# Norms, 1x1 convolutions and a sparse mixture of experts: logits in eight 64x32 tiles over two banks, a spread per piece of the logits, a ring of five pieces, and the sums of steps 0, 2, 5 and 6 at other places

## Chip, cores and metric

One NeuronCore of one Trainium2 chip runs the kernel. The metric is device time in microseconds (us), of a whole execution.

## The reference

The input `x` is 8 images of 64 channels by 128x128 pixels, all fp32. First a convolution block, whose FFT and inverse cancel out:

```
xc = layernorm over channels of x
xn = groupnorm(8 groups)(xc) * gn_w + gn_b
x1 = x + xc + w2 @ relu(w1 @ xn + b1) + b2          # 1x1 convolutions
```

Then a sparse mixture. The reference reads x1 as (batch 8, tokens 16384, 64), normalizes each token over its channels, and computes

```
logits = tokens @ gate_w.T + gate_b                 # 32 experts
probs  = softmax over the 16384 tokens of an image
top 8 tokens of each expert, pooled with their probabilities
each expert's two-layer gelu network on the pooled vector
x1 += expert output * probability, at the chosen tokens
```

## The kernel before

**Layout.** An image lies in SBUF as 128 partitions (two halves of the pixels, `h`, times 64 channels) by 8192 columns, in `xs[it % 2]`. It is worked on in eight units `u` of 1024 columns (two slices `sl` of 512, each of two parts `sub` of 256). Two units make a group `m` for sums, and two units make a piece of the logits.

**Rounds and steps.** The main loop has eight rounds `it` of eight steps `s`. Every engine runs its own `step(it, s)`, in program order, and waits on semaphores. In round `it`, image `it` goes through its convolutions, image `it` + 1 is normalized (C jobs: subtract the mean; S jobs: multiply by the reciprocal deviation), and of image `it` - 1 the logits are scaled and the best tokens are found (L jobs in rounds 1 to 7, E jobs for the last image).

**PE in a step.** `conv1` (L383) of unit `s`; eight transposes into the two banks of `tl` (L400, for the stored tokens) of the unit before; a spread (L494); sums over channels; `conv2` (L391); a spread; the logits (L409) of the unit before; further sums. `spread_at(it, (s, j))` is the j-th spread of a step. A spread is four matmuls that copy a row of statistics over partitions into the two banks `bc`; DVE multiplies or subtracts it (L938, L940, L936) and only then may the next spread be written.

**Sums.** `sum_group` (L372) sums a group over the channels with 8 matmuls of 128x32 tiles: `x_sums` of the input and `xc_square_sums` of ACT's squares for the first norm, `x1_sums` and `x1_square_sums` for the token norm. The last waits for `sqx_done`, ACT's squares of x1 (L781). The square sums of group 1 need units 0 to 3 squared, and stood in step 5.

**The other engines.** DVE: statistics, the multiplies, `x1` (L948: adds the residual to `conv2`'s result), `max` and `max_index` of each piece (L1030, L1035), candidates (L1042 ff.). ACT: relu (L761), copies of tokens (L766) and logits (L776), squares (L794, L801, L781), exponentials (L806). POOL: adds (L1426), and gathers and scatters at the end. SP: loads and stores. ACT's order in a step:

```
relu(it, par, s)
square_at(it, (s - 1, 2));  explog(...);  token_copy(b, u)
square_at(it, (s, 0))
square_x1(b, b % 2, u)
logits_copy(b, u)
square_at(it, (s, 1))
```

with `u` = `s` - 1 for `s` from 1 on. `square_at(it, (4, 0))` is the square of the S0 job, which waits for DVE's multiply of S0. SP loads group `m` of image `it` + 2 in step 2m + 3 once `grp_done` says that the sums of squares of that group are done, and stores each unit's tokens after ACT's copy. In the prologue DVE builds constants, among them `spread`, while the first load is under way. After the loop come the last image's top tokens and the expert networks.

## Time and profile before

| | |
|---|---|
| median of 3 runs | 632.74 us (632.73 to 635.37) |
| the profiled execution | 639.6 us, span 637.9 us |
| mean granted TensorE clock | 0.935 |
| `x1` of step 0 in rounds 3, 4, 5, 6 | 248.65, 313.86, 379.05, 444.24 us |

The sums of the prediction are made against the profiled execution. The steps of round 4, by PE's start of `conv1`, and how long three engines were busy in each:

| step | from us | length | PE | DVE | ACT |
|---|---|---|---|---|---|
| 0 | 308.30 | 9.35 | 8.22 | 6.88 | 6.89 |
| 1 | 317.65 | 8.20 | 7.38 | 7.58 | 5.97 |
| 2 | 325.85 | 8.54 | 7.35 | 7.17 | 5.22 |
| 3 | 334.39 | 8.48 | 8.25 | 7.19 | 7.57 |
| 4 | 342.87 | 9.36 | 7.62 | 9.15 | 6.26 |
| 5 | 352.23 | 7.60 | 6.56 | 7.29 | 7.28 |
| 6 | 359.83 | 7.27 | 6.93 | 5.78 | 7.27 |
| 7 | 367.10 | 6.39 | 6.19 | 5.31 | 5.30 |

An engine that is busy for all of a step sets its length; where none is, the step is a chain of waits among them. The granted clock is 1.00 in all of these steps.

### The profile page before, as it was taken

How to read it: one execution, taken by the hardware profiler on the slowest of the kernel's cores; microseconds unless marked ns; L12 is line 12 of the kernel's file. 1: busy time of each engine (PE TensorE's matmuls, PEld its weight loads, DVE VectorE, ACT ScalarE, POOL GpSimd, SP SyncE). 2: the span in 40 equal slices, each digit the busy share in tenths (PEclk: the TensorE clock that was granted, in tenths of full speed). 3: DMA queues.
4: the chain of work that ended last, by engine and by line, in shares of the span. 5: the costliest groups of instructions: out<-in, count | busy, mean ns of one | idle time of the engine just before them, and what ended most of it. 6: DMA issues, size and time to landing. Idle time of an engine off the chain costs nothing.

```text
span 637.9 us, 14170 instructions
## 1 busy us (share of the span) xinstructions
PE 535.4 (84%) x5732; PEld 270.3 (42%) x5732; DVE 487.2 (76%) x950; ACT 435.3 (68%) x651; POOL 189.6 (30%) x116
## 2 busy tenths in 40 slices
PE   2749999898998899889989899989887988876982
PEld 1324444444444344444444444444443433434762
DVE  5574556689888988898789878988888687799620
ACT  2463779677976797679767976797677855984110
POOL 1007435023502260217020802080207145121144
PEclk9955999999999999999999999999998998987595
DMA  8960144714471447244634454445401255430000
GB/s 195 195 144 0 68 133 142 188 68 133 133 199 67 134 133 191 76 133 134 168 98 134 115 160 123 133 101 165 133 35 67 76 182 154 146 100 5 6 15 19
DMA packets 26752, 73.38 MB, mean 115 GB/s; under 512 B 4152, under 2 KB 4152, under 8 KB 22592
## 3 DMA queue, kind: packets, MB, share of 16 engines
q1 hardware_dynamic: 25664, 71.44, 40.9%
q0 software_dynamic: 1024, 1.05, 0.6%
q8 instruction: 45, 0.74, 0.5%
q14 instruction: 19, 0.16, 0.1%
HBM read 38.40 MB, written 34.08 MB: 114 GB/s over the span
## 4 chain that ended last, share of the span: by engine, by line
PE 41%; DVE 30%; ACT 13%; issue 12%; DMA 2%; POOL 1%; SPq 0%; ACTq 0%; DVEq 0%; POOLq 0%
PE st L372 11%; ACT junk L801 7%; DVE xs L948 7%; PE cv L383 6%; PE cv L391 6%; PE tl L400 6%; PE bc L494 5%; DVE us L938 5%; DVE lg L936 3%; DVE top_i L1035 2%; ACT tok L766 2%; DVE us L940 2%; DVE cnd L1030 2%; DMA xs<-in_x 2%; PE tl L409 2%
## 5 line engine op out<-in xcount | busy, mean ns | idle before, releaser
L1426 POOL TENSOR_TENSOR xs<-xs,us 128x1024 f32<-128x1024 f32 x64 | 151.2, 2379 | 367.2 <-DVE xs L948 173.4
L948 DVE SCALAR_TENSOR_TENSOR xs<-cv,vecs,xs 128x1024 f32<-128x1024 f32 x64 | 82.1, 1282 | 47.8 <-PE cv L391 47.7
L794 ACT ACTIVATE sqc<-us 128x1024 f32<-128x1024 f32 x64 | 67.5, 1054 | 46.2 <-DVE us L938 45.4
L761 ACT ACTIVATE hid<-cv,b1n 128x1024 f32<-128x1024 f32 x64 | 71.2, 1113 | 36.5 <-PE cv L383 36.0
L938 DVE TENSOR_TENSOR us<-xs,bc 128x1024 f32<-128x1024 f32 x60 | 73.0, 1216 | 19.7 <-PE bc L494 19.3
L400 PEld LDWEIGHTS tl<-ident,xs 128*128 128x128 f32 x512 | 63.8, 195 | 53.9 <-issue 53.9
L372 PE MATMUL st<-xs,stat_w 128*32 128x256 f32 x1024 | 74.5, 413 | 10.5 <-DMA xs<-in_x 9.4
L801 ACT ACTIVATE junk<-us 128x1024 bf16<-128x1024 f32 x64 | 67.3, 1051 | 22.8 <-DVE gsum L940 22.1
L940 DVE CUSTOM_DVE_ANT_0 us<-us,bc 128x1024 f32<-128x1024 f32 x60 | 72.9, 1215 | 11.2 <-PE bc L494 9.9
L400 PE MATMUL tl<-ident,xs 128*128 128x128 f32 x512 | 76.4, 294 | 0.9 <-ACT lg L776 0.9
L409 PE MATMUL tl<-xs,gcen 128*32 128x256 f32 x1024 | 69.4, 389 | 8.0 <-ACT tok L766 7.9
L494 PE MATMUL bc<-rstd_s,spread 32*128 32x256 f32 x368 | 48.2, 340 | 32.9 <-DVE gsum L940 20.3
L383 PE MATMUL cv<-us,w1n 64*64 64x512 f32 x512 | 72.1, 634 | 2.4 <-DVE b1n L1003 1.9
L391 PE MATMUL cv<-hid,w2bd 64*64 64x512 f32 x512 | 70.6, 622 | 1.0 <-ACT hid L761 1.0
L781 ACT ACTIVATE sqx<-xs 128x1024 f32<-128x1024 f32 x64 | 67.0, 1047 | 1.5 <-PE st L372 1.3
L766 ACT ACTIVATE tok<-tl 128x1024 f32<-128x1024 f32 x64 | 65.0, 1015 | 0.0
L494 PEld LDWEIGHTS bc<-rstd_s,spread 32*128 32x128 f32 x368 | 29.2, 194 | 82.2 <-DVE gsum L940 42.3
L776 ACT ACTIVATE lg<-tl 128x512 f32<-128x512 f32 x64 | 37.7, 589 | 34.4 <-PE tl L409 31.5
L494 PE MATMUL bc<-mean_s,spread 32*128 32x256 f32 x240 | 31.9, 343 | 19.5 <-DVE us L938 15.1
L372 PEld LDWEIGHTS st<-xs,stat_w 128*32 128x32 f32 x1024 | 31.1, 116 | 34.4 <-issue 14.0
L409 PEld LDWEIGHTS tl<-xs,gcen 128*32 128x32 f32 x1024 | 26.9, 110 | 38.3 <-ACT tok L766 11.5
L1030 DVE MAX8 cnd<-lg 128x8 f32<-128x1024 f32 x32 | 39.2, 1224 | 0.9
(210 smaller groups left out, 652.4 us busy)
## 6 DMA issues: line engine op xcount, KB each, us to landing
xs<-in_x SPq DMA_DIRECT2D x64, 512.0 KB, 7.0
out_rows<-tok SPq DMA_DIRECT2D x64, 512.0 KB
us<-in_e_w SPq DMA_DIRECT2D x8, 260.0 KB
xs<-in_e_w SPq DMA_DIRECT2D x8, 256.0 KB
sqc<-out_rows,idx_all POOLq DMA_INDIRECT x16
out_rows<-sqc,idx_all POOLq DMA_INDIRECT x16, 2.1
vecs<-in_b SPq DMA_DIRECT2D x4, 0.2 KB, 14.0
gate_bias<-in_gate_b SPq DMA_DIRECT2D x4, 0.1 KB, 12.3
```

The lines of the kernel that those rows point to most:

```text
L372: mm = pe.matmul(dst[32 * c:32 * c + 32], stat_w[:, q, :], src[:, col:col + SUB], start=first and m == 0 and sub == 0, stop=True, skip_gro ...
L383: mm = pe.matmul(cv[C * sl:C * sl + C, CH * h:CH * h + CH], w1n[par][r, r], half_chunk(us[par], u, h, sl), start=True, stop=True)
L391: mm = pe.matmul(cv[C * h:C * h + C, CH * sl:CH * sl + CH], w2bd[r, r], hid[r, CH * h:CH * h + CH], start=True, stop=True)
L400: mm = pe.transpose(tl[:, P * k:P * k + P], unit(xs[par], u)[:, k:UN:8], ident[:])
L409: mm = pe.matmul(lgp[NE * c:NE * c + NE, SUB * sl:SUB * sl + SUB], gcen[:, NE * h:NE * h + NE], xs[par][:, col:col + SUB], start=True, sto ...
L494: mm = pe.matmul(out[:, CH * sl + SUB * i:CH * sl + SUB * i + SUB], weights, stat[32 * c:32 * c + 32, :], start=True, stop=True)
L766: nc.scalar.activation(tok[u % 2][:].rearrange("p h t c -> p t h c"), tl[:].rearrange("p (t h c) -> p t h c", t=8, h=2), ACT.Copy).then_in ...
L801: nc.scalar.activation(junk[:], unit(us[n % 2], k), ACT.Square, accum_out=gsq[:, k:k + 1]).then_inc(usq_done, 1)
L938: ins = nc.vector.tensor_tensor(unit(us[n % 2], k), unit(xs[n % 2], k), stat[:], ALU.subtract)
L940: ins = nc.vector.tensor_tensor_reduce(unit(us[n % 2], k), unit(us[n % 2], k), stat[:], 1.0, 0.0, ALU.mult, ALU.add, gsum[:, k:k + 1])
L948: nc.vector.scalar_tensor_tensor(out=xu, in0=cv[:], scalar=vecs[:, 3:4], in1=xu, op0=ALU.add, op1=ALU.add).then_inc(x1_done, 1)
L1426: nc.gpsimd.tensor_tensor(xu, xu, su, ALU.add).then_inc(s_done, 1)
```

## The change

The logits were eight matmuls of 128 rows (one half's rows held zeros) by 32 columns, all into the first bank of `tl`. They become eight of 64 rows by 32 columns: half `h` of the pixels from its own 64 rows, into bank `h`. ACT's copy takes 256 columns from each bank. A piece of the logits now has the pixels in another order, so one L or E spread covers one whole piece (weights `spread2`, 64 rows), and two operations in `candidates` turn positions back into pixels. `spread2` takes the room of one piece: the ring has five. DVE builds it in the prologue with 32 operations. On PE, the square sums of group 3 (step 0) go from before `conv2` to before the logits; `x1_sums` of group 0 (step 2) to behind the logits and that of group 2 (step 6) to before them; the square sums of group 1 from step 5 before `conv2` to step 4, behind the logits and before the spread (4, 1), and in rounds 6 and 7 behind that spread.

```
-RING = 6
+RING = 5
...
+        spread2 = sb("spread2", [P, PIECES * 2 * P], F32R)
...
-        late = lg[:, 2 * PIECE:4 * PIECE]
+        late = lg[:, 2 * PIECE:3 * PIECE]
...
-                            c, col = 2 * sub + h, UN * u + CH * sl + SUB * sub
-                            mm = pe.matmul(lgp[NE * c:NE * c + NE, SUB * sl:SUB * sl + SUB], gcen[:, NE * h:NE * h + NE],
-                                           xs[par][:, col:col + SUB], start=True, stop=True)
+                            c, col, r = 2 * sl + sub, UN * u + CH * sl + SUB * sub, slice(C * h, C * h + C)
+                            mm = pe.matmul(lg_banks[h][NE * c:NE * c + NE, 0:SUB], gcen[r, NE * h:NE * h + NE],
+                                           xs[par][r, col:col + SUB], start=True, stop=True)
...
+                if kind in ("L", "E"):
+                    for h in range(2):
+                        for w in range(2):
+                            r, col = slice(C * w, C * w + C), P * (2 * k + h)
+                            mm = pe.matmul(bc[:, CH * w + SUB * h:CH * w + SUB * h + SUB], spread2[r, col:col + P], rstd2_s[r, :],
+                                           start=True, stop=True)
+                    mm.then_inc(bc_filled, 1)
+                    return
                 for i in range(2):
                     for sl in range(2):
-                        if kind in ("L", "E"):
-                            u = L_UNITS[k] + 2 * i
-                            c, w = 2 * (u % 2) + sl, 4 * C * (u // 2)
-                            weights, stat = spread[32 * c:32 * c + 32, w:w + 4 * C:2], rstd2_s
-                        else:
-                            c, w = 2 * (k % 2) + sl, 2 * C * (2 * (k // 2) + i)
-                            weights, stat = spread[32 * c:32 * c + 32, w:w + 2 * C], mean_s if kind == "C" else rstd_s
+                        c, w = 2 * (k % 2) + sl, 2 * C * (2 * (k // 2) + i)
+                        weights, stat = spread[32 * c:32 * c + 32, w:w + 2 * C], mean_s if kind == "C" else rstd_s
...
                 if s == 0 and b >= 0:
                     x1_sums(b, b % 2, NG - 1)
-                    x1_square_sums(b, NG - 1)
                 if s == 1 and p1:
                     xc_square_sums(n, 0)
                 if s == 2 and p1:
                     xc_square_sums(n, 1)
-                if s in (2, 4, 6):
-                    x1_sums(it, par, s // 2 - 1)
-                if s in (3, 5, 7):
+                if s == 4:
+                    x1_sums(it, par, 1)
+                if s in (3, 7):
                     x1_square_sums(it, (s - 3) // 2)
                 if s == 3 and p1:
                     xc_square_sums(n, 2)
@@ -542,8 +542,16 @@
                     spread_at(it, (s, 0))
                 else:
                     spread_at(it, (s, 1))
+                if s == 0 and b >= 0:
+                    x1_square_sums(b, NG - 1)
+                if s == 6:
+                    x1_sums(it, par, 2)
                 if b >= 0:
                     logits(b, b % 2, u)
+                if s == 2:
+                    x1_sums(it, par, 0)
+                if s == 4 and n + 1 < NB:
+                    x1_square_sums(it, 1)
                 if s == 4:
                     spread_at(it, (s, 1))
                 if s == NU - 1 and p1:
@@ -555,6 +563,8 @@
                     xc_square_sums(n, 3)
                 if s in (4, 6) and n + 1 < NB:
                     x_sums(n + 1, s // 2 - 2)
+                if s == 4 and n + 1 >= NB:
+                    x1_square_sums(it, 1)
                 spread_at(it, (s, 2))
...
-                    pe.wait_ge(tok_done, NU * NB)
+                    pe.wait_ge(lcopy_done, NU * NB)
...
-                nc.scalar.activation(lg[:, col:col + CH], lgp, ACT.Copy).then_inc(lcopy_done, 1)
+                nc.scalar.activation(lg[:, col:col + CH].rearrange("p (h r) -> p h r", h=2),
+                                     tl[:].rearrange("p (h r) -> p h r", h=2)[:, :, 0:SUB], ACT.Copy).then_inc(lcopy_done, 1)
...
-                    u = L_UNITS[k]
                     if kind == "E":
                         t = NB - 1
-                    dve.wait_ge(lcopy_done, NU * t + u + 3)
-                    lt = lg[:, place(t, u // 2):place(t, u // 2) + 2 * PIECE]
-                    lt = lt.rearrange("p (i w sl r) -> p w i sl r", i=2, w=2, sl=2)[:, u % 2]
-                    ins = nc.vector.tensor_tensor(lt, lt, bc_l, ALU.mult)
+                    dve.wait_ge(lcopy_done, NU * t + 2 * k + 2)
+                    ins = nc.vector.tensor_tensor(piece(t, k), piece(t, k), bc[:], ALU.mult)
...
-                for k in range(2 * (i // 2), 2 * (i // 2) + 2):
-                    dve.wait_ge(bc_used, scaled(t, k))
+                dve.wait_ge(bc_used, scaled(t, i))
...
-                link(nc.vector.tensor_scalar(top_hi[:], top_i[:], 0xFFFFFF00, None, ALU.bitwise_and))
+                link(nc.vector.tensor_scalar(top_hi[:], top_i[:], 0xFFFFFE00, None, ALU.bitwise_and))
                 link(nc.vector.scalar_tensor_tensor(out=pix, in0=top_i[:], scalar=rowoff[:], in1=top_hi[:],
                                                     op0=ALU.add, op1=ALU.add))
+                link(nc.vector.tensor_scalar(top_hi[:], top_i[:], SUB, None, ALU.bitwise_and))
+                link(nc.vector.scalar_tensor_tensor(out=pix, in0=top_hi[:], scalar=float(HW // SUB - 1), in1=pix,
+                                                    op0=ALU.mult, op1=ALU.add))
                 link(nc.vector.tensor_tensor(pix, pix, pixbase[:], ALU.add))
...
+            for q in range(4):
+                r = slice(32 * q, 32 * q + 32)
+                for k in range(PIECES):
+                    both = spread2[r, 2 * P * k:2 * P * (k + 1)].rearrange("p (h sl b e) -> p sl h b e", h=2, sl=2, b=2)
+                    picked = tb[r, 4 * k:4 * k + 4].rearrange("p (b h) -> p h b", b=2).unsqueeze(3).broadcast_to([32, 2, 2, NE])
+                    nc.vector.tensor_copy(both[:, q % 2], picked)
+                    nc.vector.tensor_scalar(both[:, 1 - q % 2], picked, 0.0, None, ALU.mult)
```

## Rows read from the trace of the kernel before

**Rows 1.** The page, part 1: busy us, share of the span, instructions.

```profile
PE 535.4 (84%) x5732; PEld 270.3 (42%) x5732; DVE 487.2 (76%) x950; ACT 435.3 (68%) x651; POOL 189.6 (30%) x116
```

**Rows 2.** Windows, steps 5 and 6 of round 4: length, busy us, PEclk.

```profile
352.23:359.83 7.60, 6.56 (x70) 3.10 (x68) 7.29 (x12) 7.28 (x12) 7.14 (x4) 1.00 0.18 63
359.83:367.10 7.27, 6.93 (x83) 3.31 (x81) 5.78 (x11) 7.27 (x13) 4.35 (x2) 1.00 0.80 204
```

**Rows 3.** Timeline of PE: start, us, engine, line, output<-input, passes.

```profile
314.15 1.07 PE L409 MATMUL tl<-xs,gcen 128*32 128x256 f32 x16
315.04 1.05 PE L372 MATMUL st<-xs,stat_w 128*32 128x256 f32 x16
...
342.87 1.09 PE L383 MATMUL cv<-us,w1n 64*64 64x512 f32 x8
343.88 1.16 PE L400 MATMUL tl<-ident,xs 128*128 128x128 f32 x8
344.97 1.07 PE L372 MATMUL st<-xs,stat_w 128*32 128x256 f32 x16
345.97 1.09 PE L391 MATMUL cv<-hid,w2bd 64*64 64x512 f32 x8
```

**Rows 4.** Groups by shape: busy us, mean ns | idle before.

```profile
L776 ACT ACTIVATE lg<-tl 128x512 f32<-128x512 f32 x64 | 37.7, 589 | 34.4 <-PE tl L409 31.5 <-remote 2.8
```

**Rows 5.** Timeline of DVE, candidates in round 4.

```profile
366.87 0.18 DVE L1042 TENSOR_SCALAR top_hi<-top_i 128x32 uint32<-128x32 uint32 x1
...
367.37 0.19 DVE L1045 TENSOR_TENSOR cnd<-cnd,pixbase 128x32 f32<-128x32 f32 x1
```

**Rows 6.** Timeline of all engines in the prologue.

```profile
5.72 0.29 DVE L1260 TENSOR_TENSOR w1n<-ident,w1n 128x128 f32<-128x128 f32 x1
...
10.78 0.42 DVE L955 CAST hi<-st 128x256 fp32r<-128x256 f32 x1 [4.76 <-PE st L372]
...
13.37 1.93 PE L372 MATMUL st<-xs,stat_w 128*32 128x256 f32 x16 [0.70 <-DMA xs<-in_x]
```

**Rows 7.** Timeline of DVE and of ACT in step 0 of round 4.

```profile
313.86 1.28 DVE L948 SCALAR_TENSOR_TENSOR xs<-cv,vecs,xs 128x1024 f32<-128x1024 f32 x1 [1.58 <-PE cv L391]
...
315.86 1.21 DVE L938 TENSOR_TENSOR us<-xs,bc 128x1024 f32<-128x1024 f32 x1
...
313.28 0.37 ACT L811 ACTIVATE ta<-st 128x256 f32<-128x256 f32 x1
```

**Rows 8.** Timeline of PE in step 2 of round 4.

```profile
329.27 1.05 PE L372 MATMUL st<-xs,stat_w 128*32 128x256 f32 x16
...
333.96 0.50 PE L494 MATMUL bc<-mean_s,spread 32*128 32x256 f32 x4 [1.19 <-DVE us L938]
```

**Rows 9.** Timeline of DVE and of ACT, steps 4 and 5 of round 4.

```profile
350.53 1.21 DVE L940 CUSTOM_DVE_ANT_0 us<-us,bc 128x1024 f32<-128x1024 f32 x1
...
349.44 1.06 ACT L801 ACTIVATE junk<-us 128x1024 bf16<-128x1024 f32 x1 [2.27 <-DVE gsum L940]
...
350.50 1.04 ACT L781 ACTIVATE sqx<-xs 128x1024 f32<-128x1024 f32 x1
...
353.39 1.12 ACT L761 ACTIVATE hid<-cv,b1n 128x1024 f32<-128x1024 f32 x1 [0.33 <-PE cv L383]
```

**Rows 10.** Timeline of PE in step 4 of round 4.

```profile
349.47 0.50 PE L494 MATMUL bc<-rstd_s,spread 32*128 32x256 f32 x4 [0.90 <-DVE gsum L940]
```

**Rows 11.** Timeline of PE in step 6 of round 7.

```profile
551.09 1.07 PE L372 MATMUL st<-xs,stat_w 128*32 128x256 f32 x16 [1.09 <-DVE lnv L1013]
```

**Rows 12.** Timeline of PE after two idle times, rounds 6 and 7.

```profile
482.53 0.50 PE L494 MATMUL bc<-rstd_s,spread 32*128 32x256 f32 x4 [1.83 <-DVE gsum L940]
482.96 1.72 PE L383 MATMUL cv<-us,w1n 64*64 64x512 f32 x8
...
533.01 0.51 PE L494 MATMUL bc<-rstd_s,spread 32*128 32x256 f32 x4 [2.09 <-issue]
...
534.47 1.97 PE L400 MATMUL tl<-ident,xs 128*128 128x128 f32 x8
```

More of the change, by code:

```diff
@@ L51 @@
 M_JOB, LAST_M_JOB = (7, 0), (7, 1)
-L_UNITS = (0, 1, 4, 5)
 VALUES_AT = {1: 0, 2: 1, 3: 2, 4: 3}
@@ L191, in mk_metaformer_kernel @@
         eq = xs[0][:, HW // 2:HW].rearrange("p (b f i) -> p b f i", b=NB, f=GATHERS)
-        late = lg[:, 2 * PIECE:4 * PIECE]
+        late = lg[:, 2 * PIECE:3 * PIECE]
         pool_f = late[:, 0:NE * NB + 3 * NB]
-        diags = [eq[:, 7 - p % 2].rearrange("p f i -> p (f i)") for p in range(3)] + [late[:, 2 * CH:3 * CH]]
+        diags = [eq[:, 7 - p % 2].rearrange("p f i -> p (f i)") for p in range(3)] + [sqx[:, CH:2 * CH]]
         hg = us[1][:, 0:4 * CH]
@@ L199, in mk_metaformer_kernel @@
         id2 = gcen
-        sel = late[:, 3 * CH:3 * CH + 2 * P].rearrange("p (b k e) -> p b k e", b=2, k=4)
+        sel = late[:, CH:CH + 2 * P].rearrange("p (b k e) -> p b k e", b=2, k=4)
         outs8 = us[1][:, 0:CH].rearrange("p (e c) -> p e c", e=8)
@@ L209, in mk_metaformer_kernel @@
         lgp, pt = tl[:, 0:CH], tl[:, CH:2 * CH]
+        lg_banks = (lgp, pt)
         first_banks = [bc, cv]
@@ L255, in mk_metaformer_kernel @@
         out_ts = [o.rearrange("(h u p t) c -> u p h (t c)", h=HALVES, u=NU, p=P) for o in outs]
-        RSTD_STEPS, GN_STEPS, LN2_STEPS, TOP_STEPS, MRG_STEPS = 4, 7, 5, 11, 11
+        RSTD_STEPS, GN_STEPS, LN2_STEPS, TOP_STEPS, MRG_STEPS = 4, 7, 5, 13, 11
         def unit(buf, u, ring=NU):
@@ L265, in half_chunk @@
             return buf[C * h:C * h + C, UN * u + CH * sl:UN * u + CH * sl + CH]
-        bc_l = bc[:].rearrange("p (sl i r) -> p i sl r", sl=2, i=2)
         def place(b, i):
@@ L1192, in token_norm @@
                 zz = zs.rearrange("p b g c -> p (b g) c")[:, n0:n1]
-                q = late[:, CH:CH + (n1 - n0) * C].rearrange("p (n c) -> p n c", c=C)
+                q = sqx[:, 0:(n1 - n0) * C].rearrange("p (n c) -> p n c", c=C)
                 mean, var, y, a, rs, ws = (tr[:, i, n0:n1] for i in range(6))
@@ L1231, in _ @@
             for r in range(4):
-                nc.vector.memset(rowoff[32 * r:32 * r + 32, :], float(SUB * (r // 2) + HW * (r % 2)))
+                nc.vector.memset(rowoff[32 * r:32 * r + 32, :], float(SUB * r))
             nc.vector.memset(gt[:, 10:11], EPS_C)
```

## Prediction

> **What bounds the kernel now.** The page comes first: the engine shares show PE busy for 84% of the span, DVE 76%, ACT 68% [rows 1], and the chain of work that ended last is handed round among all three. So no share of busy time answers the question; it has to be read step by step. The table of steps above gives one round of the loop (`it` = 4, 65.2 us). In steps 5 and 6 ACT is busy 7.28 of 7.60 us and 7.27 of 7.27 us [rows 2]: there ACT is the bound, and PE work taken out is worth nothing. In steps 0 to 4 the bound changes hands at each wait, which the timeline of PE, DVE and ACT shows.
>
> **The logits.** Eight matmuls of 128 rows by 32 columns (16 passes in the trace) take 0.89 us from their start to the start of sums that follow [rows 3]. In four column tiles they need two turns; in eight tiles of 64x32, one. Nearest row for tiles of two row halves running together: four 64x64 matmuls of 512 columns, 1.02 us for one turn from 342.87 to 343.88 [rows 3], so one turn of 256 columns is half the streaming, some 0.45 us, and about 0.1 more for the change of tile shape: 0.55 us, a gain of 0.35 (bounds: 0 if the halves don't overlap, 0.45). Rows show that 0.1: logits, 16 passes of 256 columns, take 0.89 us before sums of the same tile shape, and sums, as many passes of as many columns, 1.00 us before `conv2` in another [rows 3]. 
> ACT's copy now reads two half-filled banks, 512 columns as before: 0.59 us [rows 4], taken as unchanged (the larger copies read two banks too; at worst 0.05 us x 64 = 3 us, at best nothing). A gain of 0.35 x 64 = 22 us would need PE to be the bound everywhere, which the steps deny.
>
> **Spreads, ring, candidates.** A spread is still four matmuls in two row tiles and DVE's multiply still covers 128x1024: 0. It scales one piece in place of parts of two, and the order on DVE is the same: 0. The ring of five lets the copy of a piece wait for the piece exponentiated in that same step, which ACT does earlier in its own order: 0. Two more linked DVE operations per batch cost 0.5 us, as the same two kinds do from 366.87 to 367.37 [rows 5]. In rounds 1 to 6 DVE then waits 0.6 us for ACT's last square, which hides them; without that cover they'd cost 3 us. The last batch has them on the chain: +0.5.
>
> **The prologue.** `spread2` is built by 32 small DVE operations of 32x128. DVE is idle for 4.76 us before its first mean [rows 6]. A 128x128 operation of that stretch lasts 0.29 us [rows 6]; with the overlap of unlinked ones I take 0.20 us each (0.15 would fit the idle time, 0.29 is the other bound): they take 6.4 us, 1.7 us too much; the transfer that PE awaits for its second group leaves 0.70 us of cover [rows 6]. I take +1.2, bounds 0 and +3.8.
>
> **Steps 0 to 2.** Step 0: the square sums leave the place before `conv2` (1.0 us), so `x1` at 313.86, which waited 1.58 us for `conv2` [rows 7], comes 0.9 us earlier. But ACT's L811 needs the square sums, which now end 1.5 us later, at about 314.35: 0.37 for L811 [rows 7] and 0.80 for DVE's two variance operations (315.06 to 315.86, ahead of the last of those rows), and the subtract that stood at 315.86 [rows 7] starts at 315.6: gain 0.25 of 0.9. SP's load of group 3 needs the logits as well, which come 0.3 earlier. Step 2: `x1_sums` at 329.27 goes from before `conv2` into PE's wait of 1.19 us before 333.96 [rows 8]. `conv2` comes 1.0 + 0.25 earlier, the `x1` behind it too, and all to the end of step 3 is DVE and PE in turn: the round is 1.2 us ahead when S0 is multiplied (bounds 0.9 and 1.5).
>
> **Step 4, the core of it.** The square sums of units 2 and 3 now stand on PE between the logits and the spread S1. They wait for `sqx_done` of unit 3. ACT squares unit 3 only behind the square of S0, and that waits for DVE's S0. The rows: ACT waits 2.27 us for DVE's S0, starts its square at 349.44 and unit 3's at 350.50, which ends at 351.54 [rows 9]. Before, PE began to spread S1 at 349.47, behind a gap of 0.90 us [rows 10], and DVE took S1 at 350.53 [rows 9]. Now: sums 351.58, spread S1 351.58 + 0.89 = 352.47, filled at 352.97, DVE's S1 at 353.0 against 350.53: 2.45 us late. Behind the waiting PE instruction stand S1, the sums of the next batch, S2 and `conv1` of step 5. S2's spread waits for S1's multiply, `conv1` comes behind it, and ACT's relu at 353.39 opens a stretch in which ACT never rests [rows 2, 9]. So the 2.45 us go through whole, and the sums taken from step 5 (1.00 us) and moved in step 6 give nothing back. POOL's adds and SP's loads have slack (POOL 4.35 of 7.27 us in step 6 [rows 2]; SP's step-5 load waits for a token copy, not for these sums).
> Net per round 2.45 - 1.2 = +1.25 us; five rounds (1 to 5): +6.25.
> Round 0 has no scaled logits and its steps 5 and 6 are led by PE, so it gets the 1.00 us back: -1.5 + 2.45 - 1.0 = about 0. Round 6 has the sums behind S1: +0.7, less 1.3 before: -0.6. Round 7: no C or S work; step 0 gives 0.9, step 5 some 0.9, and the sums that held `conv2` until 551.09 [rows 11] leave it, but ACT's relu and token copy lead there, 0.7: -2.5 in all (bounds -1 and -4), before the +0.5 above.
>
> **The clock.** PE's new wait runs from about 348.05 to 351.58: 3.5 us with no work, where it had one of 0.9 us. The trace has two like it. In round 6 PE stood idle for 1.83 us before 482.53 and the granted clock fell: the `conv1` that follows lasts 1.72 us where 1.09 is usual; after 2.09 us of idle before 533.01 the transposes last 1.97 for 1.16 [rows 3, 12]. So I expect the lower level (1.2 GHz) in four of five rounds. If it covers the sums and a spread that costs 0.9 + 0.3 us, if `conv1`, 0.63: 0.9 us on average, 4 x 0.9 = +3.6 (bounds 0 and 9).
>
> **The sum.** 1.2 + 0 + 6.25 - 0.6 - 2.5 + 0.5 + 3.6 = +8.4 us. It is made against the profiled execution (span 637.9, its time 639.6 us), which would become some 648; that execution is 6.9 us above the median of the runs, 632.74, so the forecast is 632.7 + 8.4 = 641.
>
> **Rivals.**
> A, the clock stays up: the same stall without the 3.6 us, 637.5. For it: the sums follow at once and PE is dense before the gap. Against: 2.09 us were enough once.
> B, faster, by a catch-up behind step 4: if PE rather than ACT leads steps 5 and 6, the sums taken out of each give 1.0 + 1.0 us back in five rounds, and with the clock up the sum is 1.2 + 6.25 - 10 - 0.6 - 2.5 + 0.5 = -5.2: 627.5. It decides from about 1.5 us of ACT idle in those two steps; the rows show 0.3 us.
> C, the gains weigh more: if the new sums start earlier, because ACT's squares don't wait as in round 4, the stall is 1.5 us and the clock stays up: 4.8 - 5 x 0.95 = 0, 633. Against: the order on ACT is fixed and S0 comes from DVE.
> D, the change doesn't do what it says: the two row halves take turns and logits stay at 0.89 us. The stall is as forecast, and each round loses some 0.3 of its gain: 643.
>
> **Chances.** Forecast 0.45 (its own range 637 to 647), A 0.22, B 0.12, C 0.13, D 0.08. Within 0.5% (629.6 to 635.9) is about what a measurement of this kernel can't tell from no change. B is faster, 0.12; C with a little of A is no change, 0.15; the rest slower, 0.73. The range is 630 to 649: up to the clock's and the prologue's bounds on one side, down to C on the other, with B left out.
>
> **What would show it.** In step 4 of rounds 1 to 5: PE waits some 3.5 us for ACT's square at L781, DVE waits about 2.4 us for S1's spread, and the period of a round goes from 65.2 to 66.5 us or more. In step 2 the 1.19 us wait is gone. L409 falls from 0.89 to about 0.55 us per unit. The granted clock falls below 1.00 around step 5. Wrong would be: ACT idle in steps 5 and 6 yet no time lost, unit 3 squared before S0, or a shorter round.

## The result and the profile after

The changed kernel takes 654.48 us (median of 4 runs, 653.74 to 655.45), against 633.44 us (4 runs, 632.73 to 635.37) for the kernel before beside it: a ratio of 1.0328, 95% interval 1.031 to 1.0346. The forecast was 641.0 us with a range of 630 to 649. The direction is right, and the loss of 21.0 us is two and a half times the 8.4 us forecast, above the range.

The page after, its parts 1 and 2: busy us, share, instructions; then tenths of 40 slices.

```profile
span 652.0 us, 14188 instructions
...
PE 530.6 (81%) x5732; PEld 255.3 (39%) x5732; DVE 494.1 (76%) x998; ACT 435.7 (67%) x651; POOL 188.5 (29%) x116
...
PEclk9855989997899889998999799989998998987595
```

(PE is TensorE, DVE VectorE, ACT ScalarE, POOL GpSimd; PEclk is TensorE's granted clock.) PE is busy for 4.8 us less than in [rows 1], in a span that is 14.1 us longer. The mean granted clock went from 0.935 to 0.904.

One of the costliest groups on the page after: line, engine, operation, count | busy us, mean ns | idle before, and whom it waited for.

```profile
L948 DVE CUSTOM_DVE_ANT_0 us<-us,bc 128x1024 f32<-128x1024 f32 x60 | 73.0, 1217 | 38.6 <-PE bc L495 37.4
```

DVE's multiply of the S jobs now waits 38.6 us in all for PE's spreads; before it was 11.2 us. Step 4 of round 4 shows where that arises. PE's timeline after: start, us, line, output<-input, passes, idle before and releaser.

```profile
352.91 1.09 PE L381 MATMUL cv<-us,w1n 64*64 64x512 f32 x8
...
357.12 0.50 PE L495 MATMUL bc<-rstd_s,spread 32*128 32x256 f32 x4
357.55 0.66 PE L407 MATMUL tl<-xs,gcen 64*32 64x256 f32 x16
361.65 1.30 PE L370 MATMUL st<-sqx,stat_w 128*32 128x256 f32 x16 [3.44 <-ACT sqx L792]
362.88 0.79 PE L495 MATMUL bc<-rstd_s,spread 32*128 32x256 f32 x4
363.60 1.93 PE L370 MATMUL st<-xs,stat_w 128*32 128x256 f32 x16
365.47 0.79 PE L495 MATMUL bc<-rstd_s,spread 32*128 32x256 f32 x4
366.19 1.98 PE L381 MATMUL cv<-us,w1n 64*64 64x512 f32 x8
368.11 1.60 PE L398 MATMUL tl<-ident,xs 128*128 128x128 f32 x8
369.63 0.50 PE L495 MATMUL bc<-rstd_s,spread 32*128 32x256 f32 x4
```

And ACT and DVE there:

```profile
359.50 1.06 ACT L812 ACTIVATE junk<-us 128x1024 bf16<-128x1024 f32 x1 [2.28 <-DVE gsum L948]
...
360.55 1.04 ACT L792 ACTIVATE sqx<-xs 128x1024 f32<-128x1024 f32 x1
...
363.72 1.22 DVE L948 CUSTOM_DVE_ANT_0 us<-us,bc 128x1024 f32<-128x1024 f32 x1 [3.06 <-PE bc L495]
```

This is the stall of the forecast: the square sums stand on PE ahead of S1's spread and wait for ACT's third square, which stands behind S0's square. They start 8.74 us after the step's `conv1` (361.65 less 352.91); the forecast had 8.71 (351.58 less 342.87). What was not seen in its size is what follows. From 361.65 to 369.63 PE does, without a pause and in 7.98 us, two groups of sums, two spreads, `conv1` and the transposes; by [rows 3] and the spreads' 0.43 us that is 1.0 + 0.43 + 1.0 + 0.43 + 1.0 + 1.1 = 5.0 us of work. The windows say why (length, busy us of PE, PEld, DVE, ACT, POOL, then PEclk):

```profile
358.00:360.00 2.00, 0.21 (x8) 0.00 (x0) 1.97 (x4) 0.50 (x1) 0.46 (x1) 1.00 0.73 268
360.00:362.00 2.00, 0.35 (x8) 0.27 (x12) 0.66 (x1) 2.00 (x4) 1.90 (x1) 1.00 0.02 2
362.00:364.00 2.00, 2.00 (x24) 0.85 (x19) 0.28 (x1) 0.08 (x1) 0.00 (x0) 0.59 0.00 0
364.00:366.00 2.00, 2.00 (x20) 0.89 (x12) 2.00 (x4) 1.02 (x2) 0.97 (x1) 0.50 0.00 0
366.00:368.00 2.00, 2.00 (x12) 0.30 (x8) 1.97 (x5) 0.13 (x2) 1.77 (x2) 0.50 0.00 0
368.00:370.00 2.00, 2.00 (x16) 1.71 (x12) 0.67 (x1) 1.76 (x2) 1.98 (x1) 0.71 0.01 4
```

PE stood nearly idle for 4 us, and then the granted clock was 0.50 (1.2 GHz) while it worked at 100%, over six groups of matmuls, where the forecast had priced one or two.

The length of each round in the two profiled executions, from PE's first `conv1` of step 0 to the next round's:

| | start | 0 | 1 | 2 | 3 | 4 | 5 | 6 | 7 | tail |
|---|---|---|---|---|---|---|---|---|---|---|
| before | 51.32 | 61.86 | 64.70 | 65.20 | 65.22 | 65.20 | 65.19 | 67.06 | 48.84 | 83.3 |
| after | 50.15 | 63.22 | 68.84 | 69.45 | 67.85 | 68.82 | 67.81 | 66.36 | 46.04 | 83.5 |
| difference | -1.2 | +1.4 | +4.1 | +4.3 | +2.6 | +3.6 | +2.6 | -0.7 | -2.8 | +0.1 |

The sum is +14.1, as the spans say. The medians differ by 21.0, because the profiled execution of before (639.6 us) lay 6.2 us above the median of its four runs (6.9 above that of the three that the forecast had), and the one of after 0.7 below its own. Most of the 6.2 can be placed. The start of the loop scatters from 49.02 to 51.34 us over the fourteen profiles of this document. Of the four experiments that issue the same work up to there as the kernel before, with its 51.32, three start at 49.0 to 49.5 (2, 8 and 11) and one at 51.34 (9): up to 2.3 us. And in round 7, steps 3 to 5 last 22.67 us in the profile of before and 19.55 in the eighth experiment, which issues the same work in them: the spread that waited 2.09 us in [rows 12], for nothing that the profile shows, waits 1.09 us there, and no slow transposes follow.

```profile
526.29 0.51 PE L494 MATMUL bc<-rstd_s,spread 32*128 32x256 f32 x4 [1.09 <-DVE lg L941]
...
527.75 1.16 PE L400 MATMUL tl<-ident,xs 128*128 128x128 f32 x8
```

That is 3.1 us, and with the start up to 5.4 of the 6.2. Steps 0 to 3 of rounds 1 to 5 agree within 0.03 us between the profiles of before and of the second experiment, so rounds 1 to 5 can be compared.

### The profile page after: what moved, and what is told of

Its sections match the earlier page's. It is cut to its first block, busy times and chain, and to the rows that moved or that the text cites. A ratio compares the mean times of both kernels' runs of the same rounds, so it can differ in the third digit from the quotient of the medians.

```text
span 652.0 us, 14188 instructions
## 1 busy us (share of the span) xinstructions
PE 530.6 (81%) x5732; PEld 255.3 (39%) x5732; DVE 494.1 (76%) x998; ACT 435.7 (67%) x651; POOL 188.5 (29%) x116
## 4 chain that ended last, share of the span: by engine, by line
PE 41%; DVE 28%; ACT 14%; issue 13%; POOL 3%; ACTq 0%; DVEq 0%; POOLq 0%
PE st L370 12%; PE cv L381 7%; ACT junk L812 6%; PE tl L398 6%; PE bc L495 5%; PE cv L389 5%; DVE us L946 5%; DVE xs L956 4%; DVE lg L944 4%; POOL out_rows L1476 2%; ACT tok L776 2%; DVE top_i L1042 2%; DVE cnd L1037 2%; ACT hid L771 1%; ACT sqx L792 1%
## 5 line engine op out<-in xcount | busy, mean ns | idle before, releaser
L948 DVE CUSTOM_DVE_ANT_0 us<-us,bc 128x1024 f32<-128x1024 f32 x60 | 73.0, 1217 | 38.6 <-PE bc L495 37.4
L370 PE MATMUL st<-xs,stat_w 128*32 128x256 f32 x1024 | 78.7, 431 | 8.4 <-DMA xs<-in_x 8.3
L381 PE MATMUL cv<-us,w1n 64*64 64x512 f32 x512 | 75.1, 658 | 5.0 <-DVE b1n L1011 5.0
L370 PE MATMUL st<-sqx,stat_w 128*32 128x256 f32 x512 | 38.8, 425 | 21.7 <-ACT sqx L792 21.7
L407 PE MATMUL tl<-xs,gcen 64*32 64x256 f32 x1024 | 42.9, 392 | 10.1 <-ACT tok L776 10.1
L495 PE MATMUL bc<-rstd_s,spread 32*128 32x256 f32 x240 | 34.4, 368 | 16.0 <-DVE gsum L948 12.5
L370 PEld LDWEIGHTS st<-xs,stat_w 128*32 128x32 f32 x1024 | 29.4, 119 | 41.0 <-issue 25.8
L495 PEld LDWEIGHTS bc<-rstd_s,spread 32*128 32x128 f32 x240 | 20.8, 214 | 51.2 <-DVE gsum L948 33.5
L944 DVE TENSOR_TENSOR lg<-lg,bc 128x1024 f32<-128x1024 f32 x32 | 38.8, 1214 | 0.7 <-PE bc L487 0.6
```

Source lines behind the costliest of these rows:

```text
L370: mm = pe.matmul(dst[32 * c:32 * c + 32], stat_w[:, q, :], src[:, col:col + SUB], start=first and m == 0 and sub == 0, stop=True, skip_gro ...
L381: mm = pe.matmul(cv[C * sl:C * sl + C, CH * h:CH * h + CH], w1n[par][r, r], half_chunk(us[par], u, h, sl), start=True, stop=True)
L495: mm = pe.matmul(out[:, CH * sl + SUB * i:CH * sl + SUB * i + SUB], weights, stat[32 * c:32 * c + 32, :], start=True, stop=True)
```

## The experiments

Two theories stood after the result. T: two things cost, the stall, and a lower clock wherever PE's steps have become too thin, by the stall or by the shorter logits. The rival, called W in the first expectations: the stall and its clock are all, and the tiles are neutral or a gain. S, a third, is that the tile shapes, the spread per piece or the ring cost time by themselves. Kernel 1 is the kernel of experiment 1, and so on. "Slow stretches" below are my count, in rounds 0 to 6 of the profiled execution, of places where sums last over 1.25 us or a convolution or transposes over 1.4 us; before has 1, after has 8; the granted clock is 0.50 in each. The ratios are to the kernel before on the same chip (632.5 to 636.8 us, medians 634.05, 634.57, 633.81, 634.52).

**1. The square sums of group 1 back in step 5.** The rest of the change stays.

```
-                if s in (3, 7):
+                if s in (3, 5, 7):
                     x1_square_sums(it, (s - 3) // 2)
...
-                if s == 4 and n + 1 < NB:
-                    x1_square_sums(it, 1)
...
-                if s == 4 and n + 1 >= NB:
-                    x1_square_sums(it, 1)
```

> The changed kernel with one edit undone: the square sums of group 1 stand in step 5 ahead of conv2 again. Theory W (the wait of those sums on PE in step 4, with the clock that falls behind it, is the whole loss): in the profile of the changed kernel steps 4 and 5 of rounds 1 to 5 are 2.6 to 4.9 us longer than before, while steps 0 to 2 are 1.2 us shorter; without the wait 654.5 - 27 = about 628, granted clock back at 0.93 or more. Rival S (the new tile shapes, the spread per piece or the ring cost the time): stays near 654. Rival T (the shorter logits leave PE thinner, and the clock falls for that): between, 640 to 650, with the clock still near 0.90.

Measured 637.33 us, 1.0052 (1.0031 to 1.0073), 6 slow stretches. The stall is gone and 17 us come back, but not the 27 that W expected; 637 lies between W and T. Step 4 is at 9.4 to 9.7 us again in rounds 1 to 5; in round 2, step 5 lasts 10.17 us, in round 3 step 6 lasts 8.34. PE's timeline at the first of these:

```profile
214.35 0.66 PE L407 MATMUL tl<-xs,gcen 64*32 64x256 f32 x16
216.32 0.50 PE L495 MATMUL bc<-rstd_s,spread 32*128 32x256 f32 x4 [1.31 <-DVE gsum L944]
...
218.65 0.79 PE L495 MATMUL bc<-rstd_s,spread 32*128 32x256 f32 x4 [0.83 <-DVE gsum L944]
```

The wait ahead of S1's spread was 0.90 us in [rows 10]; the shorter logits add 0.4 to it. It costs nothing by itself: the spread starts 6.62 us after the step's `conv1` (216.32 less 209.70), against 6.60 before (349.47 less 342.87).

**2. That move alone**, in the kernel before.

```
-                if s in (3, 5, 7):
+                if s in (3, 7):
                     x1_square_sums(it, (s - 3) // 2)
...
+                if s == 4 and n + 1 < NB:
+                    x1_square_sums(it, 1)
                 if s == 4:
                     spread_at(it, (s, 1))
...
+                if s == 4 and n + 1 >= NB:
+                    x1_square_sums(it, 1)
```

> The kernel before with only the square sums of group 1 moved to step 4, as the change does (rounds 6 and 7 behind the spread). Theory W: 633.4 + 27 = about 660, more than the whole change, because nothing gives back. Rival S: within 3 us of 633. Rival T: the wait alone without the shorter logits, 633 + 6 x 2.45 = 648 and a clock near 0.93.

Measured 659.57 us, 1.0404 (1.0378 to 1.0431), 6 slow stretches, one in each of rounds 1 to 6. One instruction group in another place costs 25.5 us, more than the whole change, as W had expected. PE's timeline in step 4 of its round 4:

```profile
360.83 1.07 PE L409 MATMUL tl<-xs,gcen 128*32 128x256 f32 x16
364.93 1.93 PE L372 MATMUL st<-sqx,stat_w 128*32 128x256 f32 x16 [3.03 <-ACT sqx L785]
...
367.52 1.93 PE L372 MATMUL st<-xs,stat_w 128*32 128x256 f32 x16
...
370.10 1.66 PE L383 MATMUL cv<-us,w1n 64*64 64x512 f32 x8
```

**3. ACT squares unit 3 ahead of S0's square**, in the changed kernel.

```
+                if s == 4:
+                    square_x1(b, b % 2, u)
                 square_at(it, (s, 0))
-                if s >= 1:
+                if s >= 1 and s != 4:
                     square_x1(b, b % 2, u)
```

> The changed kernel, with ACT squaring unit 3 of x1 ahead of S0's square in step 4, in a stretch where ACT was idle for 2.27 us; PE's order is that of the change. Theory W: the sums find their squares at once, S1's spread is on time, the sums of step 5 are gone: 626 to 630, as with the sums put back or 1 to 2 us less through round 0. If the position on PE itself costs (a delay of S1 behind 0.9 us of sums), 633 to 636. Rivals S and T: 645 or more.

Measured 630.21 us, 0.9937 (0.9913 to 0.9962): 24 us from the order of two ACT instructions, since ACT had waited 2.28 us there anyway. This shows what caused the stall. Step 4 is at 9.37 and step 5 at 7.3 us, but step 6 at 8.5 in five rounds, with 7 slow stretches. PE's windows across the end of step 5 in round 4:

```profile
352.00:354.00 2.00, 0.92 (x20) 0.48 (x20) 2.00 (x4) 2.00 (x4) 1.96 (x2) 1.00 0.00 0
354.00:356.00 2.00, 1.23 (x20) 0.55 (x12) 2.00 (x4) 2.00 (x5) 2.00 (x2) 0.89 0.78 253
356.00:358.00 2.00, 2.00 (x11) 0.69 (x4) 1.46 (x4) 1.59 (x3) 1.84 (x2) 0.50 1.12 284
```

And its timeline there:

```profile
352.69 0.50 PE L495 MATMUL bc<-rstd_s,spread 32*128 32x256 f32 x4 [0.88 <-DVE gsum L950]
353.58 0.67 PE L407 MATMUL tl<-xs,gcen 64*32 64x256 f32 x16 [0.39 <-ACT tok L776]
355.02 0.50 PE L495 MATMUL bc<-rstd_s,spread 32*128 32x256 f32 x4 [0.77 <-DVE gsum L950]
355.44 1.94 PE L381 MATMUL cv<-us,w1n 64*64 64x512 f32 x8
```

There is no long wait here: waits of 0.88, 0.39 and 0.77 us and PE busy about half of 4 us came before the fall.

**4. The stall with PE kept busy.** The changed kernel, the logits of step 4 issued five times more in rounds 0 to 5, into columns that nothing reads.

```
-                    logits(b, b % 2, u)
+                    logits(b, b % 2, u, 5 if s == 4 and n + 1 < NB else 0)
```

> The changed kernel with the logits of step 4 computed five more times in rounds 0 to 5, into columns of the two banks that nothing reads, so that PE works through the wait of 3.5 us. The stall stays, the clock should not fall. If the stall costs 2.45 us a round as forecast and the clock the rest (4.6 - 2.45 = 2.15 us a round), 654.5 - 6 x 2 = 642 to 643, with the granted clock at 0.93. If the clock costs 0.9 us as forecast, 649. If the clock is not the cause of the slow matmuls behind the wait, 654 or more.

Measured 647.22 us, 1.0186 (1.0144 to 1.0229). Step 4 lasts 12.0 us in rounds 1 to 5, against 9.36 before, with the clock at 1.00 in rounds 2 to 5: the bare stall is 2.64 us a round (2.45 forecast). PE in round 4; L414 are the repeats:

```profile
354.68 2.37 PE L414 MATMUL tl<-xs,gcen 64*32 64x256 f32 x80
358.31 1.07 PE L370 MATMUL st<-sqx,stat_w 128*32 128x256 f32 x16 [1.27 <-ACT sqx L799]
```

By the time alone, 647.22 is nearer to the 649 of the forecast's price for the clock than to 642 to 643. The profile says why: the clock still falls, later, in step 6 of most rounds (8.5 to 10.3 us), so the filling was less than half of a cure. Round 3 is the one without a slow stretch from its start to its end, and it lasts 66.66 us against 65.22: that is what a round loses to the stall, less its gains, 1.44 us.

**5. Kernel 1 with more PE work**: the logits of steps 4 and 5 issued once more in rounds 0 to 5.

> The changed kernel with the square sums of its second group back in step 5 (that gave 637.3 us, and its clock still fell in step 5 of some rounds), and now with the sixteen logit matmuls of steps 4 and 5 issued once more each in rounds 0 to 5, into columns of their tile that nothing reads; it adds work and leaves nothing out. Theory T (the small logit tiles made TensorE's steps thinner, and in some rounds the clock of the stretch before S1's convolutions falls for that): the repeats lie in TensorE's idle time, the clock stays at its upper level, steps 4 and 5 last 9.4 and 9.1 us in every round, and the time is 624 to 627. Rival (the falls come from the place of the sums or from step 6, not from thin logits): 637 again, or some us above it for the added matmuls.

Measured 631.16 us, 0.9913 (0.9874 to 0.9952), 3 slow stretches in place of 6. Added work made it 6 us faster than kernel 1 by the medians, with intervals apart, and between the two expectations. The clock still fell in step 5 of rounds 3, 5 and 6, where step 5 lasted 8.8 to 10.1 us.

**6. Kernel 3 with the logits of step 5 issued once more** in rounds 0 to 5.

> The changed kernel with the third unit's squares put on ScalarE before S0's square in step 4 (that gave 630.2 us, with step 6 at 8.5 us where 7.3 would do, at a clock that fell), and now the logits of step 5 issued once more in rounds 0 to 5 into columns that nothing reads. If thin logits in step 5 let the clock fall at its end: step 6 goes to 7.3 us, 6 rounds times 1.2 less, 623. If step 6 is slow for another reason: 630.

Measured 626.66 us, 0.9871 (0.9846 to 0.9897). Step 6 is at 7.3 to 7.7 us in rounds 1 and 2 and still at 8.5 in 3 to 5: half of the effect expected.

**7. The tiles half alone**: 64x32 logits, spread per piece, ring of five, with every sum at its old place.

```
                 if s == 0 and b >= 0:
                     x1_sums(b, b % 2, NG - 1)
+                    x1_square_sums(b, NG - 1)
...
-                if s == 4:
-                    x1_sums(it, par, 1)
-                if s in (3, 7):
+                if s in (2, 4, 6):
+                    x1_sums(it, par, s // 2 - 1)
+                if s in (3, 5, 7):
```

> Only the tiles half of the change: logits by 64x32 tiles, spread per piece, ring of five, with every sum at its place of before. Theory T (shorter logits alone let the clock fall in steps with a wait in them): 636 to 641, granted clock under 0.93, and conv1 matmuls of about 1.9 us in steps that have 1.0 us ones in the kernel before. Rival (the tiles are neutral, since TensorE waits for the chains in every step anyway): 631 to 634, clock as before.

Measured 657.47 us (651.7 to 661.18), 1.033 (1.028 to 1.0381). Even T had expected only 636 to 641. Less work on PE, nothing moved, and 22.9 us lost. The profiled execution, 661.18 us, is the slowest of the four; it has 17 slow stretches and a clock of 0.881. In step 2 of round 2:

```profile
205.97 0.66 PE L407 MATMUL tl<-xs,gcen 64*32 64x256 f32 x16
208.23 0.64 PE L495 MATMUL bc<-mean_s,spread 32*128 32x256 f32 x4 [1.60 <-DVE us L937]
208.81 1.98 PE L381 MATMUL cv<-us,w1n 64*64 64x512 f32 x8
210.72 1.63 PE L398 MATMUL tl<-ident,xs 128*128 128x128 f32 x8
```

The wait for DVE was 1.19 us in [rows 8] and is 1.60 here, by the 0.3 to 0.4 us that the logits no longer take; the spread behind it starts 8.12 us after the step's `conv1` (208.23 less 200.11), as before (333.96 less 325.85 is 8.11). So the longer wait by itself delays nothing. The work after it runs at the lower clock, and step 3 lasts 9.8 to 10.0 us in place of 8.5. The whole change moves `x1_sums` into just that wait, of which 0.60 us are left, and its step 3 lasts 8.5 us:

```profile
344.01 0.50 PE L495 MATMUL bc<-mean_s,spread 32*128 32x256 f32 x4 [0.60 <-DVE us L946]
```

**8. The moves of steps 0, 2 and 6 alone**, in the kernel before; logits and group 1 as they were.

```
                     x1_sums(b, b % 2, NG - 1)
-                    x1_square_sums(b, NG - 1)
...
+                if s == 0 and b >= 0:
+                    x1_square_sums(b, NG - 1)
+                if s == 6:
+                    x1_sums(it, par, 2)
                 if b >= 0:
                     logits(b, b % 2, u)
+                if s == 2:
+                    x1_sums(it, par, 0)
```

> The kernel before, its logits unchanged, with only the sums of steps 0, 2 and 6 at the places of the change; the square sums of the second group stay in step 5. The gain of steps 0 to 2 was 1.16 us a round in the changed kernel's profile, 0.9 to 2 us in rounds 0 and 7. If it belongs to the moves and the clock stays up: 634 less 6 x 1.1 less 0.9 less 2 = 624.5. If the gain of those steps needs the shorter logits too: 632 to 634.

Measured 629.39 us, 0.9915 (0.9891 to 0.9939). That is between the two expectations. Rounds 2, 3 and 5 last 64.13 us against 65.2: the moves gain 1.07 a round without the shorter logits. Round 4 lasts 67.15, with step 5 at 10.32 us. PE there:

```profile
342.42 0.50 PE L494 MATMUL bc<-rstd_s,spread 32*128 32x256 f32 x4 [0.89 <-DVE gsum L945]
...
344.75 0.80 PE L494 MATMUL bc<-rstd_s,spread 32*128 32x256 f32 x4 [0.83 <-DVE gsum L945]
345.48 1.99 PE L383 MATMUL cv<-us,w1n 64*64 64x512 f32 x8
```

Rounds 2, 3 and 5 have the same two waits and no slow stretch. The profile doesn't show what decides which round falls.

**9. All moves, unit 3 squared first, the old logits.** Kernel 3 without its tiles half: kernel 8 with the edits of 2 and 3.

> The kernel before with all the moves of the change (steps 0, 2, 4, 5 and 6) and the third unit's squares ahead of S0's square on ScalarE; its logits by 128x32 tiles, 0.89 us each, as before. It is the kernel that gave 630.2 us without the tiles half of the change. Theory T (short logits thin out TensorE's steps and cost clock; nothing else of the tiles costs or gains much): 625 to 629, and step 6 of rounds 3 to 5 at 7.3 in place of 8.5 us. Rival (the tiles gain something of their own once no wait stands in step 4): 631 to 634.

Measured 628.89 us, 0.9916 (0.9886 to 0.9947), 3 slow stretches in place of 7. The tiles' share is within the error here (0.9937 with them, intervals overlapping). Step 6 is at 7.6 us and not 8.5 in four of rounds 1 to 5, but 9.39 in round 3, and in rounds 4 and 5 the clock falls in step 5 instead (7.99 us in place of 7.27).

**10. The tiles half with as much PE time for the logits as before.** Kernel 7, with half of each unit's logits issued once more, in every step.

```
                for _ in range(fill):
                    for sub in range(2):
                        for h in range(2):
                            c, col, r = sub, UN * u + SUB * sub, slice(C * h, C * h + C)
                            mm = pe.matmul(lg_banks[h][NE * c:NE * c + NE, SUB:2 * SUB], gcen[r, NE * h:NE * h + NE],
                                           xs[par][r, col:col + SUB], start=True, stop=True)
```

> Only the tiles half of the change (that gave 657.5 us), with half of each unit's logits issued once more into columns that nothing reads, so that the logits take TensorE 0.88 us again in every step, in the new tiles; it adds work and leaves nothing out. If the missing TensorE work is what lowered the clock: 632 to 638, clock 0.93. If it is something else of the tiles half (the spread per piece, the order of the pieces, the ring of five, the change of tile shape): 655 to 660 as without the repeats.

Measured 637.25 us (635.87 to 637.36), 1.0047 (1.0027 to 1.0068), clock 0.933, 3 slow stretches. Half a unit's logits that nobody reads give 20.2 of the 22.9 us back. The wait in step 2 of round 2 is 1.20 us again and the clock stays up:

```profile
200.89 0.61 PE L413 MATMUL tl<-xs,gcen 64*32 64x256 f32 x8
202.70 0.50 PE L501 MATMUL bc<-mean_s,spread 32*128 32x256 f32 x4 [1.20 <-DVE us L943]
203.13 1.09 PE L381 MATMUL cv<-us,w1n 64*64 64x512 f32 x8
```

That spread, too, starts 8.12 us after `conv1`. So all but 3.4 us of the loss is the missing PE work, and not the tile shape, the spread per piece or the ring; 3.4 us (interval 1.0027 to 1.0068) are left, in rounds 1 and 4 with a slow stretch in step 5 and in some 0.25 us a round of steps 1 and 6. One thing isn't separated: the repeats also put the signal for ACT's copy of the logits back to its old time.

**11. Kernel 9 with the first half of step 5's logits issued twice more**, same values, same place.

> All moves with the third unit's squares first and the old logits, and in rounds 0 to 5 the first half of step 5's logits issued twice more, with the same values into the same place (0.9 us more TensorE work in a step in which it waits for ScalarE and VectorE). If the clock that falls at the end of step 5 is what makes step 6 last 8.5 us: step 6 at 7.0 to 7.3 in all rounds, 622 to 625. If the repeats only push the spread behind them: as the same kernel without them, or up to 6 x 0.5 = 3 us slower.

Measured 626.85 us (622.17 to 628.67), 0.9861 (0.9817 to 0.9905). Step 6 is at 7.35 us in all of rounds 1 to 5, near the 7.0 to 7.3 expected, but in two of them step 5 itself lasts 9.37 in place of 7.70; in round 5 the repeated logits last 3.61 us there. The fall moved forward into the work that was meant to prevent it:

```profile
414.90 0.50 PE L494 MATMUL bc<-rstd_s,spread 32*128 32x256 f32 x4 [0.88 <-DVE gsum L951]
415.80 3.61 PE L409 MATMUL tl<-xs,gcen 128*32 128x256 f32 x32 [0.40 <-ACT tok L775]
```

The runs don't tell this kernel from kernel 9: the intervals overlap.

**12. Kernel 5 with the square sums of step 5 behind `conv2`.**

```
-                if s in (3, 5, 7):
+                if s in (3, 7):
                     x1_square_sums(it, (s - 3) // 2)
...
                     conv2(it, s)
+                if s == 5:
+                    x1_square_sums(it, 1)
```

> The changed kernel with the square sums of its second group in step 5, but behind conv2, where TensorE waits 0.87 us for the multiply ahead of S4's spread, and with the logits of steps 4 and 5 issued once more in rounds 0 to 5 into columns that nothing reads. The same work with the sums before conv2 gave 631.2 us, and its rounds lasted 63.5 to 65.6, with step 5 at 8.8 us where the clock fell. If conv2 1.0 us earlier closes the gaps of step 5: step 5 at 7.3 to 7.5 in every round, 622 to 625. If the wait only moves to the relu that follows conv2, or the clock falls as before: 627 to 631.

Measured 627.28 us (6 runs, 624.18 to 629.04), 0.9892 (0.9871 to 0.9913). Step 5 still lasts 8.1 to 8.4 us in five of rounds 1 to 6. That is the second expectation: the clock falls as before.

The fastest are kernels 6, 11 and 12, which the runs don't tell apart: 1.1 to 1.4% below the kernel before, 4% below the changed one.

## Why the prediction was wrong

In the order of its steps, with the terms of its sum:

| term | forecast | measured, profiled executions |
|---|---|---|
| prologue | +1.2 | -1.2 (start of the loop) |
| round 0 (forecast without a clock term) | about 0 | +1.4 |
| rounds 1 to 5, stall less gains | +6.25 | about +7.4 |
| rounds 1 to 5, clock | +3.6 | about +9.9 |
| round 6 | -0.6 | -0.7 |
| round 7 | -2.5 | -2.8 |
| tail | +0.5 | +0.1 |

**The logits.** Forecast 0.55 us; they take 0.59 from their start to that of the sums behind them (341.75 to 342.34 in step 2 of round 4). The change did what it says, so rival D is out. By the Trainium skill (TensorEngine Tiling (Array Packing), Key Properties) a change of tiling mode drains TensorE; 0.59 for one turn, where half of the 1.02 us of [rows 3] is 0.51, leaves room for it; the page gives no duration, the 0.1 us of the forecast came from the row alone, and no run isolates it. ACT's copy reads two banks in 588 ns, as before [rows 4].

**The prologue.** The 32 operations start 0.14 us apart and take from 4.28 to 8.99 us; the first mean starts at 10.79, against 10.78 in [rows 6]. Their cover held, and the cost is 0. The term was too large by 1.2. (Its own figures, 6.4 less 4.76 less 0.70, give 0.9.) The -1.2 of the table is no gain: the loop starts between 49.02 and 51.34 us in the profiles without `spread2`, and between 49.20 and 51.00 in those with it.

**Steps 0 to 2.** A gain of 1.2 a round was forecast; steps 0 to 2 of round 4 took 24.93 us against 26.09, so 1.16. Experiment 8 gives 1.07 of it to the moves. The wait of step 2 isn't gone, as was forecast, but down to 0.60 us.

**Step 4.** The mechanism, its place, its start (8.74 for 8.71) and its size (2.64 for 2.45, experiment 4) were right. That nothing is given back behind it was right in the sum: in round 3 of experiment 4, which has no slow stretch, step 5 is 0.34 us shorter than before and steps 6 and 7 are 0.31 longer. The 1.44 us that this round loses stand against 1.25 forecast. Experiment 3 shows the cause: with ACT's order changed the whole of it is gone. Rivals B and C are out: ACT's squares start no earlier, and steps 5 to 7 return nothing in all.

**The clock: this is the step that failed.** It said "0.9 us on average, 4 x 0.9 = +3.6". That the clock falls after the new wait was right, and it fell in all of rounds 1 to 5, not in four of them, and in 0 and 6 too. The size was wrong. Rounds 1 to 5 lost 17.3 us in all; less five times the stall of 2.64, and with the five gains of 1.16 put back, 17.3 - 13.2 + 5.8 = 9.9 us are left, 2.0 a round. (By the 1.44 of experiment 4's round 3 it is 10.1, and 1.2 to 2.8 in the single rounds.) The forecast had priced one or two groups of matmuls behind the wait, from `conv1` at 1.72 us in [rows 12]. In rounds 1 to 5 the slow work behind the wait is 4.0 to 8.7 us long, three to six groups, and in round 4 its six groups together last 3.0 us more. Of these about 2 stay in the round's length. The upper bound given, 9, was already too low for these five rounds. Rival A, in which the clock stays up, is out.

**What the sum did not hold at all** is that shorter logits can cost. They stood in it at nothing or a gain. Alone they cost 22.9 us (experiment 7), all but 3.4 of it by the clock (experiment 10). In the whole change this is nearly invisible: the move of group 1 costs 25.5 us alone, the other moves give 5.2, and 25.5 - 5.2 = 20.3 is already near the 21.0 measured. A likely reason is that the rest of the change filled the waits that the tiles made longer, as in step 2, and that the stall had lowered the clock anyway; no run has all the moves with the old logits and ACT's old order, which would show it. The cost of the tiles shows when the stall is removed: kernel 1 has 8 us more than kernel 8, which differs from it by the tiles half. In experiments 3 and 9 the same difference is within the error.

**Round 7, right by luck.** The -2.8 measured beside -2.5 says little. The profile of before had 3.1 us too much in steps 3 to 5 (22.67 against 19.55 in experiment 8); less these its round 7 is 45.7 us long, and the changed kernel's 46.0 are a loss of 0.3. Steps 0 and 5, forecast at 0.9 each, did give 0.75 and 1.2 (6.47 to 5.72; 6.19 in experiment 8 to 4.99), but step 4 lasts 8.33 us for 6.19: in step 3 the wait ahead of the last spread is 1.51 us, against 1.09 in experiment 8, and the clock falls behind it. Round 6's -0.7 for -0.6 has a slow stretch on either side, in step 5 before and in step 4 after.

```profile
548.29 0.50 PE L487 MATMUL bc<-rstd_s,spread 64*128 64x256 f32 x4 [1.51 <-DVE lg L944]
...
549.74 1.78 PE L398 MATMUL tl<-ident,xs 128*128 128x128 f32 x8
551.45 1.94 PE L370 MATMUL st<-xs,stat_w 128*32 128x256 f32 x16
```

**The base.** The forecast added signed differences from a profiled execution to the median of the runs. The loss by the medians is 21.0, that of the two profiles 14.1. Of the 6.9 between them 0.7 lies in the profile of after, 3.1 in round 7 of the profile of before and up to 2.3 in its start; the rest is open. So of the 12.6 us by which 21.0 passed the forecast of 8.4, the clock of rounds 1 to 5 is the largest part, 6.3 (9.9 less 3.6); round 7 less that stray time is 2.8, round 0 is 1.4, and the stall less the gains 1.1.

**What stays open.** Which of rounds 1 to 5 has a slow stretch in kernels 5, 8, 9, 11 and 12 differs with no difference in their waits that the profile shows. No version tried kept the upper clock through every round.

## What to carry to other kernels

In a kernel in which TensorE waits in every step for other engines, its idle time isn't free to enlarge: before shortening a matmul or moving one out of a wait, look at what the granted clock does behind the waits that grow, and price a fall by all the work of the stretch that follows (here 1.2 to 2.8 us of a round), not by one matmul. When an instruction is moved in its engine's order, look up where its producer stands in the order of its own engine; here the cure for the largest part of the loss was to swap two instructions there. And a change of two halves should be timed as halves, since the costs of the clock did not add up here: one half cost 22.9 us alone, the other had a part that cost 25.5 alone, and both together cost 21.0.

## What the runs showed of the hardware

Of TensorE's clock: 1.19 us of waiting in step 2 left it at 1.00 in rounds 0 to 6 of the kernel before, and 1.60 us at the same place let it fall to 0.5 in each of rounds 0 to 6 (experiment 7). It also fell without a wait over 0.9 us, after waits of 0.88, 0.39 and 0.77 us in a row (experiment 3). With waits of 0.89 and 0.83 us in step 4 it fell in round 4 and stayed up in rounds 1, 2, 3 and 5 (experiment 8); the kernel before has the same two waits in all five rounds, and in none of them did it fall. The Trainium skill (TensorE: Matmul & The Clock Gate, A second HAM failure mode: psum-queue depth-cycling) tells, of a bf16 kernel, of short idle times between groups of matmuls that make the clock swing; experiment 3's windows, in fp32, agree, with PE busy 0.92 and 1.23 of 2 us before the clock was 0.50.

Work that nobody reads made a kernel faster: 20.2 us by half a unit's logits in each step (experiment 10 against 7), 6 us by one unit's in two (experiment 5 against 1).

Eight matmuls of 64x32 tiles with 256 columns take 0.59 us where eight of 128x32 take 0.89 (start to start), and small DVE operations of 32x128, 0.21 us each, start 0.14 us apart.
